# Routing rounds, order of GpSimd's work and buffers of weighted rows, moved in a fused attention and expert kernel

## Chip, cores and metric

One core of one Trainium2 chip. The metric is the device time of one execution in microseconds; lower is better. The median of three runs of the kernel before is 2441.61 us.

## What is computed

The input x is 32 x 512 x 256 in float32. The result is x + attention(layernorm(x)) + experts(layernorm(x)), cut to what matters:

```
xn  = layernorm(x)                                  # no scale, no shift
q, k, v = xn @ Wq + bq, xn @ Wk + bk, xn @ Wv + bv  # 16 heads of 16
a   = ((q k^T) * decay_mask) v                      # no softmax; mask 0.95^(i-j), causal
att = groupnorm(a @ Wo + bo) * gamma + beta         # 16 groups over channels and tokens

probs   = softmax(xn @ gate_w)                      # 8 experts
p, idx  = top_k(probs of each batch row and expert, 128)   # of its 512 tokens
h       = gelu(xn[idx] @ w1)                        # 256 -> 1024
y       = (h @ w2) * p                              # 1024 -> 256
out     = x + att + scatter_add(y at idx)
```

## The kernel before

The kernel has two blocks, one after the other, with a barrier between them. Every engine has its own program, and semaphores order them.

**Attention block.** It runs in passes b = -2 to 32 (B = 32 batch rows). Pass b does the front of row b + 1 (projections), the scores and values of row b and the output projection, group norm and residual of row b - 1; loads and layernorm run for row b + 2. In pass 32 only the tail of row 31 is left. SyncE stores the normalised rows xn (for the experts to gather) and x plus attention. GpSimd computes the group factors from VectorE's group means; ScalarE applies them, TensorE turns the rows back, and VectorE adds the residual.

**Routing.** The gate scores of two batch rows go through a softmax in 19 small VectorE steps, ten in the odd pass and nine in the even one that follows. Sixteen batch rows times eight experts make the 128 partitions of one half of the routing. For each half TensorE turns the scores (`turn_rows`), VectorE copies them (`take_rows`), and 16 rounds (`whole_round`: top eight, their index, strike them out) find the 128 best tokens. Then the indices are made float (`as_float`), TensorE turns values and indices (`turn_top`), and VectorE copies them out (`take_top`). The first half gets one round in each of the passes 16 to 31 and its top in pass 32. The second half is turned in pass 32, gets four rounds there, three before the first expert step, five after step 0 and four after step 1.

**Expert block.** It runs 64 steps, eight experts of NG = 8 steps, each with four batch rows (GRP = 4), so 512 gathered tokens. Numbers are split in a high and a low part, three matmuls for one product, and the first layer is done with seven products instead of eight. In a step n, TensorE runs products 6, 3 and 7 (x or sums of x times w1), the transposes of the rows gathered for step n + 1, products 1, 5 and 2 of step n + 1, and in between `down`, the second layer, four row blocks k of 24 matmuls. A step has 188 matmuls. ScalarE applies the gelu, makes high parts, and weights the second layer's result (`weighted`, L1272) into `y`, one buffer of four row blocks; its first one of a step waits until the scatter of the step before has landed. VectorE adds the products (L1429) and makes low parts (g_lo L1440, xs_lo L1399). `fronts(n + 1)` are the first hidden sums of the next step with a low part of x and of g between them, from the sum of product 2 to the sum called u4B.

GpSimd's turn for step n in order: gather of the rows of step n + 1 (four indirect DMAs, L1219, once the transposes of step n are through), scatter of step n - 1 (four indirect DMAs that add to the output, L1229), and, for the next expert, one weight sum (L1185 to L1191, in four turns), the low part of a slot of w1 (L1197) and of a piece of w2 (L1204). Both low parts wait for ScalarE's high part of the same piece, which comes late in the step. The instructions of each engine run strictly in this order.

## Time and profile before

| | |
|---|---|
| median of three runs | 2441.61 us (2440.53 to 2446.41) |
| profiled execution, its own time | 2432.42 us |
| its span | 2430.6 us |
| TensorE matmul busy | 2260.1 us, 93% |
| VectorE busy | 1625.8 us, 67% |
| ScalarE busy | 1383.7 us, 57% |
| GpSimd busy | 1243.0 us, 51% |
| mean granted TensorE clock | 0.978 |

In the rows below an instruction line gives start and duration in us, engine, line of the kernel, operation, out<-in, shape and count; in square brackets stands how long the engine was idle before it and what ended that. PE is TensorE, PEld its weight loads, DVE VectorE, ACT ScalarE, POOL GpSimd. The clock is the granted share of 2.4 GHz. A line of a group ends with busy time, mean ns of one, and idle time before them with what ended it.

### The profile page before, as it was taken

The numbers are of one execution on the slowest core, as the hardware profiler recorded it, in microseconds if no ns is written. First come the engines' busy times: TensorE is split into PE (matmuls) and PEld (weight loads), VectorE is DVE, ScalarE is ACT, GpSimd is POOL, SyncE is SP. The second block draws the span as 40 slices with busy tenths as digits, with TensorE's granted clock in tenths as the row PEclk, the third lists the DMA queues.
The fourth block names the chain that finished last, engine by engine and source line by source line (L and its number), as shares of the span: only waits on it lengthen the run. The fifth ranks groups of instructions, "written<-read, shape, count | busy, mean of one in ns | idle before, by whom it ended". The sixth has DMA issues, their size and how long they took to land.

```text
span 2430.6 us, 82507 instructions
## 1 busy us (share of the span) xinstructions
PE 2260.1 (93%) x34252; PEld 2076.0 (85%) x34252; DVE 1625.8 (67%) x3170; ACT 1383.7 (57%) x2545; POOL 1243.0 (51%) x2001
## 2 busy tenths in 40 slices
PE   6999999999999955799999999999999999999997
PEld 5777777777777745799999999999999999999997
DVE  2555555566666567777677777687686787777774
ACT  4555655655555524466566566566566666656664
POOL 4444444434544323356566566565565565665553
PEclk9999999999999977899999999999999999999998
DMA  3222222222223213133233233223233333332332
GB/s 98 81 90 73 82 89 81 73 88 90 74 73 98 64 45 87 27 44 85 47 44 83 47 46 84 47 45 81 42 51 77 48 51 75 53 49 47 53 53 26
DMA packets 129351, 157.58 MB, mean 65 GB/s; under 512 B 11008, under 2 KB 118656, under 8 KB 129024
## 3 DMA queue, kind: packets, MB, share of 16 engines
q0 software_dynamic: 49152, 67.14, 17.1%
q1 hardware_dynamic: 79872, 85.54, 11.3%
q8 instruction: 272, 4.46, 0.8%
q14 instruction: 55, 0.45, 0.1%
HBM read 85.53 MB, written 67.11 MB: 63 GB/s over the span
## 4 chain that ended last, share of the span: by engine, by line
PE 47%; DVE 4%; issue 3%; DMA 3%; ACT 2%; POOL 2%; ACTq 0%; another core or an unknown queue 0%; DVEq 0%; POOLq 0%
PE y L1604 24%; PE first_products_b L1536 7%; PE first_products_a L1536 6%; PE xt L1536 6%; PE fifth_products L1536 3%; DMA out<-y,scatter_idx 2%; PE xt L1526 2%; DVE g_lo L1440 1%; POOL out L1229 1%; ACT hidden L1310 1%; DVE hidden L1429 1%; POOL xg L1219 1%; DMA xg<-xn_rows,step_idx 1%; DVE xs_lo L1399 0%; ACT x_sums L1287 0%
## 5 line engine op out<-in xcount | busy, mean ns | idle before, releaser
L1604 PE MATMUL y<-w_hi,g_hi 128*128 128x256 f32 x2048 | 582.6, 284 | 24.4 <-ACT y L1272 17.2
L1604 PE MATMUL y<-w_lo,g_hi 128*128 128x256 f32 x2048 | 572.4, 279 | 0.0
L1604 PE MATMUL y<-w_hi,g_lo 128*128 128x256 f32 x2048 | 572.2, 279 | 0.0
L1229 POOL DMA_INDIRECT out<-y,scatter_idx x256 | 427.4, 1669 | 228.5 <-ACT y L1272 136.2
L1440 DVE TENSOR_TENSOR g_lo<-hidden,g_hi 128x512 fp32r<-128x512 f32 x512 | 422.6, 843 | 3.5 <-ACT g_hi L1314 1.2
L1604 PEld LDWEIGHTS y<-w_hi,g_hi 128*128 128x128 f32 x2048 | 389.1, 190 | 30.1 <-ACT y L1272 22.5
L1310 ACT ACTIVATE hidden<-hidden 128x512 f32<-128x512 f32 x384 | 236.7, 630 | 265.1 <-DVE hidden L1429 259.0
L1604 PEld LDWEIGHTS y<-w_lo,g_hi 128*128 128x128 f32 x2048 | 387.3, 189 | 0.0
L1604 PEld LDWEIGHTS y<-w_hi,g_lo 128*128 128x128 f32 x2048 | 386.9, 189 | 0.0
L1429 DVE TENSOR_TENSOR hidden<-xt,hidden 128x512 f32<-128x512 f32 x256 | 176.1, 688 | 250.9 <-PE xt L1536 238.7
L1219 POOL DMA_INDIRECT xg<-xn_rows,step_idx x256 | 262.6, 1026 | 115.1 <-issue 59.4
L1272 ACT ACTIVATE y<-y,top_p 128x256 f32<-128x256 f32 x256 | 121.0, 473 | 149.7 <-DMA out<-y,scatter_idx 93.5
L662 DVE TENSOR_TENSOR s_sb<-scores,cst 128x1024 f32<-128x1024 f32 x128 | 149.9, 1213 | 80.5 <-PE scores L875 80.5
L1204 POOL TENSOR_TENSOR w_lo<-w_stage,w_hi 128x256 fp32r<-128x256 f32 x56 | 41.4, 739 | 259.5 <-ACT w_hi L1325 259.5
L467 POOL TENSOR_TENSOR v_parity<-v_unbiased,bv_rows 128x256 f32<-128x256 f32 x128 | 92.2, 730 | 154.5 <-ACT v_unbiased L558 152.1
L1536 PE MATMUL first_products_a<-xs_hi,w_hi 128*128 128x256 f32 x512 | 147.1, 287 | 25.5 <-DVE hidden L1429 15.4
L1314 ACT ACTIVATE g_hi<-hidden 128x512 fp32r<-128x512 f32 x256 | 161.9, 633 | 6.2
L1429 DVE TENSOR_TENSOR hidden<-first_products_a,hidden 128x512 f32<-128x512 f32 x128 | 88.1, 689 | 97.8 <-PE first_products_a L1536 52.7
L1536 PE MATMUL first_products_b<-xs_hi,w_hi 128*128 128x256 f32 x512 | 144.6, 282 | 6.6 <-DVE hidden L1429 5.4
L1536 PE MATMUL first_products_b<-xs_hi,w_lo 128*128 128x256 f32 x512 | 143.2, 280 | 0.0
L1536 PE MATMUL first_products_a<-xs_lo,w_hi 128*128 128x256 f32 x512 | 143.0, 279 | 0.0
L1536 PE MATMUL first_products_a<-xs_hi,w_lo 128*128 128x256 f32 x512 | 143.0, 279 | 0.0
(190 smaller groups left out, 6182.3 us busy)
## 6 DMA issues: line engine op xcount, KB each, us to landing
x<-in_x SPq DMA_DIRECT2D x32, 512.0 KB, 5.2
w_stage<-in_w SPq DMA_DIRECT2D x16, 1024.0 KB
xn_rows<-xn SPq DMA_DIRECT2D x32, 512.0 KB, 3.2
res<-in_x SPq DMA_DIRECT2D x32, 512.0 KB, 3.8
out<-res SPq DMA_DIRECT2D x32, 512.0 KB, 3.5
xg<-xn_rows,step_idx POOLq DMA_INDIRECT x256
out<-y,scatter_idx POOLq DMA_INDIRECT x256
cst<-in_cst SPq DMA_DIRECT2D x1, 436.0 KB, 4.5
```

The lines of the kernel that those rows point to most:

```text
L467: pool.tensor_tensor(own, spread(vraw[:, t, 0:D]), spread(bv[:]), ALU.add).then_inc(vm_ready, 1)
L662: dve.tensor_tensor(s_sb[z][:, banks, :].rearrange("p k (g i) -> p (k g) i", i=SUB), sbk[:, banks, :].rearrange("p k (g i) -> p (k g) i", ...
L1219: pool.indirect_dma_start(xg[k][:], None, xn_d, bass.IndirectOffsetOnAxis(idx[:, k:k + 1], 0)).then_inc(gathered, 16)
L1229: pool.indirect_dma_start(out_rows, bass.IndirectOffsetOnAxis(sidx[:, k:k + 1], 0), y[:, k, :], None, compute_op=ALU.add).then_inc(scatter ...
L1272: act.activation(y[:, k, :], yb[k % 2][:, 0:D], ACT.Copy, scale=p_v[:, bass.ds(g * GRP + k, 1), bass.ds(e, 1)].rearrange("p a o -> p (a o) ...
L1310: act.activation(own(q, p), src, ACT.Gelu).then_inc(g_ready, 1)
L1314: act.activation(quadrant(g_hi, q, p), own(q, p), ACT.Copy).then_inc(gh_act, 1)
L1429: dve.tensor_tensor(dst, a, b, ALU.add).then_inc(sum_ready, 1)
L1440: dve.tensor_tensor(quadrant(g_lo, q, p), own(q, p), quadrant(g_hi, q, p).bitcast(F32), ALU.subtract).then_inc(gl_ready, 1)
L1526: last = pe.transpose(tb[:, h, k * P:(k + 1) * P], xg[k][:, h * P:(h + 1) * P], ident)
L1536: last = pe.matmul(dst, w_[par][:, w, cols], x__[:, x_, :], start=first and m == 0 and i == 0, stop=i == 2, skip_group_check=True)
L1604: last = pe.matmul(yb[k % 2][:, 0:D], g_[:, m, cols], w[n // NG % 2][:, m, :], start=start and m == first and i == 0, stop=end, skip_group ...
```

## The change

- The weighted rows go to two buffers in turn, the second of them the attention block's residual buffer; ScalarE waits for the scatter of two steps before (for step 1: until the attention block's last store has landed).
- GpSimd's turn n is now: scatter of step n - 1, gather of step n + 2, low part of w2 for the piece before, weight sum, low part of w1. The gather of step 1 is issued ahead of the first turn. The wait for the second half's indices moves from turn 3 to turn 2.
- The first half of the routing gets two rounds in the passes 20 and 25, so it is through in pass 29, and its top is taken in pass 30.
- Pass 31 does both parts of the last softmax ahead of its residuals, turns the second half's rows at its end and does two rounds; pass 32 does two after its first split, and three after the group means. Three more stand before the first expert step as before, and three in each of the steps 0 and 1, now ahead of `fronts`.
- ScalarE's inner loop over the steps of an expert is written out.

```diff
-    LAST_PASS_ROUNDS = 4
+    TWICE = (4, 9)
+    LAST_PASS_ROUNDS = (2, 2, 3)
-    STEP_ROUNDS = (5, 4)
+    STEP_ROUNDS = (3, 3)
...
+        TOP_AT = B - 2
...
+            def rounds(part):
+                n = Routing.LAST_PASS_ROUNDS
+                for r in range(sum(n[:part]), sum(n[:part + 1])):
+                    route.whole_round(dve, 1, r)
...
                 if has(a):
                     for s in range(2):
                         a_split(a, s)
+                if b == B:
+                    rounds(1)
...
-                if b == B:
+                if b == TOP_AT:
                     route.as_float(dve, 0)
-                    route.take_top(dve, 0, sbk[:, 0, :])
-                if b in (MID, B):
+                if b == MID:
                     softmax(b, par)
...
+                if b == TOP_AT:
+                    route.take_top(dve, 0, sbk[:, 0, :])
                 if b == B:
-                    route.take_rows(dve, 1, sbk[:, 2, :])
-                    for r in range(Routing.LAST_PASS_ROUNDS // 2):
-                        route.whole_round(dve, 1, r)
+                    rounds(2)
...
-                if 0 <= g < Routing.ROUNDS:
-                    route.whole_round(dve, 0, g)
+                if 0 <= g < TOP_AT - MID:
+                    r = g + sum(t < g for t in Routing.TWICE)
+                    route.whole_round(dve, 0, r)
+                    if g in Routing.TWICE:
+                        route.whole_round(dve, 0, r + 1)
...
+                if b == B - 1:
+                    softmax(b, par)
+                    softmax(B, 0)
                 if has(a):
                     for j in range(2):
                         residual(a, j)
-                if b not in (MID, B):
+                if b not in (MID, B - 1, B):
                     softmax(b, par)
                 if has(f):
                     states(f, fp)
-                if b == B:
-                    for r in range(Routing.LAST_PASS_ROUNDS // 2, Routing.LAST_PASS_ROUNDS):
-                        route.whole_round(dve, 1, r)
+                if b == B - 1:
+                    route.take_rows(dve, 1, sbk[:, 2, :])
+                    rounds(0)
...
+                    if b == TOP_AT:
+                        pe.wait_ge(route.chosen, 2)
...
-        y = sb("y", [P, GRP, D])
+        y = [sb("y", [P, GRP, D]), res]
...
             gather(0, 0, 0)
+            gather(0, 1, 1)
...
                 for g in range(NG):
-                    if first and g == NG // 2 - 1:
-                        pool.wait_ge(route.chosen, 4)
-                    if g < NG - 1:
-                        gather(e, g + 1, n0 + g + 1)
-                    elif not last:
-                        gather(e + 1, 0, n0 + NG)
                     if g:
                         scatter(e, g - 1, n0 + g - 1)
...
+                    if first and g == NG // 2 - 2:
+                        pool.wait_ge(route.chosen, 4)
+                    if g < NG - 2:
+                        gather(e, g + 2, n0 + g + 2)
+                    elif not last:
+                        gather(e + 1, g + 2 - NG, n0 + g + 2)
                     if g and not last:
                         if g == 1:
                             wait_apart(pool, w_in, 32 * e + 64, passed)
+                        else:
+                            low_w2(e, 1 - par, g - 1, g - 1)
                         if g <= 4:
                             weight_sum(e + 1, g)
                         low_w1(e, 1 - par, g)
-                        low_w2(e, 1 - par, g, g)
                 if not last:
+                    low_w2(e, 1 - par, NG - 1, NG - 1)
                     low_w2(e, 1 - par, 0, NG)
...
-                if k == 0:
-                    act.wait_ge(scattered, 16 * GRP * n)
+                if k == 0 and isinstance(n, int) and n == 1:
+                    act.wait_ge(out_stored, 16 * B)
+                elif k == 0 and not (isinstance(n, int) and n == 0):
+                    act.wait_ge(scattered, 16 * GRP * (n - 1))
...
-            def step(n, take, x_next):
+            def step(n, take, x_next, extra=(0, 0)):
...
                     x_sum(n + 1, 3)
+                    rounds(*extra)
                     fronts(n + 1)
...
             for n in range(Routing.TAKEN_AT):
-                step(n, False, True)
-                rounds(done, done + Routing.STEP_ROUNDS[n])
+                step(n, False, True, (done, done + Routing.STEP_ROUNDS[n]))
```

## Rows read from the trace of the kernel before

**Rows 1.** Busy time by stretch: us, PE, PEld, DVE, ACT, POOL, clock, DMA, GB/s.

```profile
100.00:863.95 763.95, 734.75 (x19917) 587.53 (x19905) 458.91 (x1108) 431.47 (x799) 339.99 (x1078) 1.00 0.26 80
863.95:921.12 57.17, 23.36 (x547) 18.48 (x547) 35.95 (x88) 12.06 (x13) 12.74 (x39) 0.62 0.22 66
921.12:1014.07 92.95, 63.48 (x476) 62.16 (x477) 72.84 (x167) 38.28 (x67) 31.13 (x29) 0.81 0.23 52
1014.07:2228.90 1214.83, 1174.68 (x9965) 1160.61 (x9965) 890.27 (x1484) 739.07 (x1372) 721.99 (x655) 0.99 0.32 57
2228.90:2381.38 152.48, 152.48 (x1319) 152.21 (x1318) 107.80 (x196) 95.59 (x172) 81.00 (x74) 1.00 0.31 49
```

**Rows 2.** Who waited for whom, 1014.07 to 2228.90 us: total, times, longest.

```profile
POOL w_lo L1204 <- ACT w_hi L1325: 248.4, 53, 7.4
...
ACT y L1272 <- DMA out<-y,scatter_idx: 82.4, 43, 5.7
...
PEld y L1604 <- ACT y L1272: 21.7, 15, 3.4
...
PEld xt L1526 <- DMA xg<-xn_rows,step_idx: 5.0, 6, 1.3
```

**Rows 3.** GpSimd's groups by form, 1014.07 to 2228.90 us.

```profile
L1229 POOL DMA_INDIRECT out<-y,scatter_idx x211 | 352.5, 1670 | 138.1 <-ACT y L1272 56.5 <-issue 53.6 <-POOL scatter_idx L1209 25.6
L1219 POOL DMA_INDIRECT xg<-xn_rows,step_idx x212 | 216.5, 1021 | 85.2 <-issue 49.3 <-POOL step_idx L1209 35.7 <-ACT y L1272 0.3
L1197 POOL TENSOR_TENSOR w_lo<-w_stage,w_hi 128x512 fp32r<-128x512 f32 x47 | 75.5, 1607 | 26.1 <-ACT w_hi L1320 25.8
L1204 POOL TENSOR_TENSOR w_lo<-w_stage,w_hi 128x256 fp32r<-128x256 f32 x53 | 39.2, 739 | 248.4 <-ACT w_hi L1325 248.4
L1191 POOL TENSOR_TENSOR w_stage<-w_stage 128x512 f32<-128x512 f32 x7 | 13.2, 1892 | 0.0
```

**Rows 4.** VectorE's groups by form, the same stretch.

```profile
L1440 DVE TENSOR_TENSOR g_lo<-hidden,g_hi 128x512 fp32r<-128x512 f32 x424 | 362.3, 871 | 2.5 <-ACT g_hi L1314 0.6
...
L1399 DVE TENSOR_TENSOR xs_lo<-x_sums,xs_hi 128x512 fp32r<-128x512 f32 x106 | 72.2, 681 | 0.0
```

**Rows 5.** ScalarE in order of time, around step 41.

```profile
1878.51 0.48 ACT L1272 ACTIVATE y<-y,top_p 128x256 f32<-128x256 f32 x1 [0.30 <-PE y L1604]
...
1893.46 0.47 ACT L1272 ACTIVATE y<-y,top_p 128x256 f32<-128x256 f32 x1 [4.24 <-DMA out<-y,scatter_idx]
```

**Rows 6.** GpSimd in order of time, the same step.

```profile
1882.70 1.63 POOL L1229 DMA_INDIRECT out<-y,scatter_idx  x1 [1.01 <-POOL scatter_idx L1209]
```

**Rows 7.** VectorE in order of time, an attention pass with a round.

```profile
589.96 0.69 DVE L675 TENSOR_TENSOR x_lo<-front,x_hi 128x512 fp32r<-128x512 f32 x1 [0.80 <-ACT x_hi L581]
```

**Rows 8.** VectorE in order of time, end of the attention block.

```profile
882.41 0.69 DVE L709 TENSOR_TENSOR res<-front,res 128x512 f32<-128x512 f32 x1 [0.16 <-PE front L974]
...
894.71 1.28 DVE L689 BATCH_NORM_STATS2 o_stats<-o 128x6 f32<-128x512 f32 x2
...
905.98 0.69 DVE L709 TENSOR_TENSOR res<-front,res 128x512 f32<-128x512 f32 x1 [0.16 <-PE front L974]
...
911.13 0.16 DVE L218 COPY topi<-best_index 128x8 uint32<-128x8 uint32 x1
```

**Rows 9.** VectorE in order of time, expert steps 0 to 2.

```profile
957.03 0.69 DVE L1429 TENSOR_TENSOR hidden<-xt,hidden 128x512 f32<-128x512 f32 x1 [4.27 <-PE xt L1536]
...
961.96 0.69 DVE L1429 TENSOR_TENSOR hidden<-first_products_b,hidden 128x512 f32<-128x512 f32 x1
...
975.38 0.68 DVE L1429 TENSOR_TENSOR hidden<-xt,hidden 128x512 f32<-128x512 f32 x1
...
991.91 0.69 DVE L1429 TENSOR_TENSOR hidden<-xt,hidden 128x512 f32<-128x512 f32 x1 [3.64 <-PE xt L1536]
...
997.33 0.68 DVE L1429 TENSOR_TENSOR hidden<-first_products_b,hidden 128x512 f32<-128x512 f32 x1
...
1009.61 0.68 DVE L1429 TENSOR_TENSOR hidden<-xt,hidden 128x512 f32<-128x512 f32 x1
```

44 lines of the change are left out of this document (23 added, 21 removed).

## Prediction

> **What bounds the kernel now.** I read the page first (busy shares, the forty slices), then busy time by stretch, then who waited for whom in the expert stage, then the engines in order of time at the places that the diff touches. Busy time by stretch [rows 1] splits the execution in five. In the attention passes and in the long expert stretch TensorE is busy 96 to 97% of the time at the full clock, so it bounds both. Between them lie two poor stretches: the end of the attention block (23.4 of 57.2 us busy, clock 0.62) and the first three expert steps (63.5 of 93.0 us, clock 0.81).
>
> The long stretch holds 53 expert steps (9965 matmul records at 188 a step): 1214.83 / 53 = 22.92 us each. The next seven steps, those of the last expert, in which no weights are prepared for a following one, take 152.48 / 7 = 21.78 us with no idle time at all [rows 1]. That is TensorE's own length of a step, the floor. So 1.14 us a step, 60.5 us in all, is lost to waits and to what they cost in clock (0.99). The waits [rows 2] name two causes directly: TensorE waits 21.7 us for ScalarE's weighted rows, which wait 82.4 us in 43 steps for the scatter of the step before to land, and 5.0 us for gathered rows. GpSimd itself waits 248.4 us in 53 steps for ScalarE's high part of w2, that is, at the end of every step, with the next gather and scatter queued behind it. In order of time: the fourth weighted rows are done at 1878.99 [rows 5], the scatter that sends them off starts only at 1882.70 [rows 6], and the next step's first weighted rows, which want the same buffer, start at 1893.46 after 4.24 us of waiting for its landing [rows 5].
>
> **The change, part by part. Two buffers for the weighted rows.** ScalarE now waits for the scatter of two steps before. A step's scatter has a whole further step of 21.8 us to land, so the 82.4 us of waiting go, and with them TensorE's 21.7 us.
>
> **GpSimd's order.** A turn is now scatter, gather for two steps on, low part of w2 for the piece before, weight sum, low part of w1. What a turn costs [rows 3]: a scatter instruction 1.67 us and (138.1 - 56.5) / 211 = 0.39 idle that is no wait for y, four times, 8.2 us; a gather 1.02 + 0.40, four times, 5.7; low parts 1.6 and 0.74; a weight sum 1.9 in four turns of an expert. That makes 18.1 us with a sum and 16.2 without, plus two small index copies, against 21.8 us of TensorE: GpSimd keeps up with about 3 us to spare. The high part of w2 that it used to wait for is by then one step old. The gather waits for the transposes of the step between; these are early in a step and the scatter ahead of it takes 8.2 us, so it lands more than ten microseconds before its rows are wanted, where before it was just in time; the 5.0 us go. Only the last two low parts of an expert still wait for ScalarE.
>
> **The low parts against VectorE.** VectorE's low parts of the activations take 871 ns on average, another subtraction of the same shape and also with both inputs in SBUF 681 ns [rows 4]; 0.19 us x 424 = 81 us are thus spent held up, and GpSimd's low parts take 1.6 us though they have only 512 columns [rows 3]. The new turn puts GpSimd's two-input operations about 14 to 18 us after the weighted rows, where VectorE waits for the second product anyway (3.6 to 4.3 us in the first steps [rows 9]). So I expect fewer collisions, not more, and with less held up VectorE the remaining waits of TensorE for hidden sums shrink too.
> The Trainium skill (SBUF — State Buffer, Who interferes with whom) says that a VectorE instruction with two SBUF inputs contends with a GpSimd instruction that reads SBUF, and that whichever starts first holds the shared pair for the whole instruction. By that rule a sum and a low part back to back can hold VectorE's subtraction for both their lengths wherever they fall, also at the newly exposed x part; the rival on collisions below is what this would be.
>
> **Size of the step term.** Bounds: nothing but the direct waits go, 21.7 + 5.0 = 26.7 us; or every step falls to the floor, 60.5 us. In between I take 21.9 us a step, nearer the floor, because it already holds in the seven steps where scatter and gather run as usual and only the weight work is missing, and ScalarE's share of that work is hidden by its idle time (739 of 1215 us busy [rows 1]): 1214.83 - 53 x 21.9 = **-54 us**.
>
> **Rounds in the first steps.** Before, five rounds stand between the end of the hidden sums at 962.65 and the next at 975.38, 12.7 us or 2.55 us a round, and four rounds and the float copies between 998.01 and 1009.61, 11.6 us [rows 9]. TensorE waits through most of both. Now the two steps get three rounds each, and ahead of the fronts, where VectorE is idle: free from 957.03 - 4.27 = 952.76, three rounds last until 960.4, 3.4 us past 957.03; in the second step from 988.27 until 995.9, 4.0 us past 991.91. From the first row of the fronts to the end of their last takes 5.6 and 6.1 us, for seven operations of 0.4 to 0.7, so one to two microseconds of waiting in them can absorb part. I take 2.5 and 3.0 late. The float copies (0.5) stay. 24.3 - 0.5 - 5.5 = 18.3, less 1 us should these shorter stalls still pull the clock down: **-17.3 us**, bounds -14 and -21.
>
> **End of attention.** The softmax halves move ahead of the last residuals of pass 31, into a wait, where the sixteenth round of the first half also used to stand. After the residual at 882.41 + 0.69 = 883.1 [rows 8] VectorE takes the rows (0.7 and up to 2 us for TensorE's transposes, I take 1), does two rounds (5.1), and only then the split of the attention output (1.3), which thus is several microseconds late and so is the output projection; two more rounds (5.1) run under the projection. The moments start at 896.3 instead of 894.71, where they had been held by softmax and copies: 1.6 late. From there the chain to the last residual is as before, so that ends at 906.67 + 1.6 = 908.3, with three rounds (7.7 us) in the wait for GpSimd's factors. Before, two rounds followed it and the block ended at 911.29 [rows 8]. **-3.0 us**, bounds 0 and -5; and seven rounds are done instead of four, which is what the first steps live on.
>
> **Attention passes.** Two passes get a second round of 2.55 us. After a round VectorE waits 0.80 us for ScalarE [rows 7] and again before the residuals, so most is hidden: 0.3 to 1 us each (if nothing hid it, 2.55 each). Taking the first half's top eight in pass 30 adds two transposes on TensorE and two short copies on VectorE, 0.5 us at most. **+1 us**, bounds 0 and +5. ScalarE's unrolled steps cost nothing that I can see: it is 61% busy in this stretch. In the last steps ScalarE's same wait goes: **-1 us**.
>
> **Sum:** +1 - 3.0 - 17.3 - 54 - 1 = -74.3 us. The profiled execution has a span of 2430.6 us (its own time is 2432.4) and the median of the runs is 2441.6, 9 us above it; I take the difference as it is: span 2356.3, median 2367.3, called 2367 us.
>
> **Rivals.**
> *Only the direct waits go.* VectorE, not ScalarE, is then what holds the fronts of a step, and TensorE's remaining 18 us of waits for hidden sums and low parts (1214.83 - 1174.68 = 40.2 us idle less 21.7) stay with their clock. For it: some steps without any scatter wait lie above the floor. Against: VectorE is 73% busy. Step term -26.7, time 2394.6.
> *Collisions move instead of going.* The sum and low part (1.9 + 1.6 us) hit the x part or the first low part of the fronts in four steps of eight, 26 steps; about 1 us left of each after slack: +26, time 2393.
> *The rounds stay exposed.* Three rounds ahead of the fronts delay the sixth product and the split waits at the end of attention, and both give back what they won: +20.3, time 2387.
> *GpSimd becomes the bound* (the other side). The gather is now behind the scatter in every turn. If instructions slow each other so that a turn passes 21.8 us, TensorE follows GpSimd's turn; slower than before in all from a turn of (1214.83 + 20.3) / 53 = 23.3 us, 5 us above my sum of 18.1. At 24 us: 53 x 24 - 1214.83 = +57, with the other terms +37, time 2478. Against: it needs every instruction a quarter longer than its mean.
>
> **Chances.** Forecast 0.69; only direct waits 0.14; collisions 0.08; rounds exposed 0.06; GpSimd bound 0.03. The forecast's own range is 2352 to 2382. The range goes to 2350 (all terms at their good ends make -86) and up to 2395, over the first three rivals. Within 0.3% (7 us), about what a measurement of this kernel can tell from no change, I give 0.02 for a mix of these, out of the forecast's share; faster 0.95, slower 0.03.
>
> **What would show it.** ScalarE's wait for the scatter gone from the waits; GpSimd's w2 low part waiting about once or twice an expert; seven-step groups of 21.8 to 22.0 us; the mean of VectorE's g_lo nearer 700 ns; clock 1.00 in the long stretch; the first three steps some 75 us long instead of 93; seven rounds before the expert block. It would be wrong if GpSimd is above 85% busy with gathers that TensorE waits for, if new waits for xs_lo appear at the sixth product in every other step, or if the passes with two rounds are over 1 us longer.

## The result, and the profile of the changed kernel

The changed kernel takes 2341.6 us (median of 4 runs, 2337.92 to 2344.88); the kernel before, run beside it, 2441.07 us (4 runs, 2439.77 to 2446.41). The ratio is 0.9588, 95% interval 0.9568 to 0.9609: 99.5 us less. The forecast of 2367 us had the direction and the mechanism, but the time fell below its range (2350 to 2395).

Busy time by stretch of the changed kernel, with the columns of [rows 1]: from 863.95 us to the first transposes of the expert block, the first three expert steps, the 53 steps after them, seven of the last expert's steps.

```profile
863.95:919.11 55.16, 22.18 (x545) 17.54 (x545) 41.68 (x104) 12.06 (x13) 12.80 (x39) 0.67 0.26 78
919.11:992.21 73.10, 61.38 (x476) 60.20 (x477) 64.58 (x144) 38.17 (x67) 27.81 (x26) 0.87 0.25 62
992.21:2142.84 1150.63, 1150.63 (x9966) 1150.63 (x9965) 810.22 (x1484) 744.89 (x1373) 750.44 (x658) 1.00 0.34 61
2142.84:2294.81 151.97, 151.97 (x1318) 151.97 (x1317) 107.06 (x196) 95.53 (x172) 83.27 (x75) 1.00 0.31 50
```

In the third line TensorE's busy time is the whole stretch. It does not wait once in 53 steps; 1150.63 / 53 = 21.71 us a step, and the seven steps behind it take the same 151.97 / 7 = 21.71. Against [rows 1], in us:

| stretch | before | after | difference | forecast |
|---|---|---|---|---|
| start to first transposes | 921.12 | 919.11 | -2.0 | +1 - 3 = -2 |
| expert steps 0 to 2 | 92.95 | 73.10 | -19.9 | -17.3 |
| 53 steps | 1214.83 | 1150.63 | -64.2 | -54 |
| 7 steps and the end | 201.7 | 200.2 | -1.5 | -1 |
| span | 2430.6 | 2343.0 | -87.6 | -74.3 |

So 13 us of the miss of 25 us are in the terms, 10 of them in the step term. The other 12 are between the two profiled executions and the medians (87.6 against 99.5), which is taken up below.

Who waited for whom in the 53 steps (engine and line, what released it; total us, times, longest):

```profile
DVE hidden L1454 <- PE xt L1561: 231.4, 53, 4.4
...
POOL out L1251 <- ACT y L1299: 144.2, 27, 8.3
POOL out L1251 <- ACT res L1299: 117.8, 26, 6.4
```

Two kinds of row that led [rows 2] are gone: GpSimd's 248.4 us for ScalarE's high part of w2 (1.1 us are left), and ScalarE's 82.4 us for the scatter. Their place is taken by GpSimd waiting for the weighted rows (262 us in the 53 steps). That idleness does no harm: GpSimd is early, and it waits for the rows that it sends off next. GpSimd's groups in the same stretch, to be held against [rows 3]:

```profile
L1241 POOL DMA_INDIRECT xg<-xn_rows,step_idx x212 | 230.3, 1086 | 85.9 <-issue 50.3 <-POOL step_idx L1231 35.6
L1251 POOL DMA_INDIRECT out<-y,scatter_idx x107 | 183.7, 1717 | 168.6 <-ACT y L1299 144.2 <-issue 21.3 <-PE xt L1551 3.0
L1251 POOL DMA_INDIRECT out<-res,scatter_idx x106 | 182.0, 1717 | 142.1 <-ACT res L1299 117.8 <-issue 21.3 <-PE xt L1551 3.0
L1219 POOL TENSOR_TENSOR w_lo<-w_stage,w_hi 128x512 fp32r<-128x512 f32 x47 | 60.9, 1295 | 0.0
L1226 POOL TENSOR_TENSOR w_lo<-w_stage,w_hi 128x256 fp32r<-128x256 f32 x53 | 39.4, 746 | 2.1 <-ACT w_hi L1351 1.1
...
L1213 POOL TENSOR_TENSOR w_stage<-w_stage 128x512 f32<-128x512 f32 x7 | 9.1, 1300 | 0.0
```

A low part of w1 takes 1295 ns and no longer 1607, a weight sum 1300 and no longer 1892. VectorE's side of it, against [rows 4]:

```profile
L1465 DVE TENSOR_TENSOR g_lo<-hidden,g_hi 128x512 fp32r<-128x512 f32 x424 | 281.1, 683 | 1.8
...
L1424 DVE TENSOR_TENSOR xs_lo<-x_sums,xs_hi 128x512 fp32r<-128x512 f32 x106 | 72.9, 688 | 0.0
```

The 0.19 us by which g_lo was longer than its like is gone. It was a mean: before, 376 of the 424 took under 0.85 us and 48 took 1.5 to 4.1 us; now the longest takes 0.70. One turn of GpSimd in order of time (start, length, engine, operation, and in brackets the idle time before it):

```profile
1790.80 1.62 POOL L1251 DMA_INDIRECT out<-y,scatter_idx  x1 [5.24 <-ACT y L1299]
...
1799.67 1.46 POOL L1241 DMA_INDIRECT xg<-xn_rows,step_idx  x1 [0.93 <-POOL step_idx L1231]
...
1805.16 0.76 POOL L1226 TENSOR_TENSOR w_lo<-w_stage,w_hi 128x256 fp32r<-128x256 f32 x1
1805.87 1.30 POOL L1219 TENSOR_TENSOR w_lo<-w_stage,w_hi 128x512 fp32r<-128x512 f32 x1
...
1812.51 1.62 POOL L1251 DMA_INDIRECT out<-res,scatter_idx  x1 [3.35 <-ACT res L1299]
```

The turn lasts 21.71 us (1790.80 to 1812.51), starting from a wait. In [rows 5] and [rows 6] the scatter began 4.2 us after the start of the fourth weighted rows; here it begins 1.3 us after the start of the rows that it sends off (1789.48, below). Those rows of before lie at a change of expert, where it was latest. Counted from the end of the fourth weighted rows, the scatters of the 53 steps began 0.80 to 6.12 us later before, 1.90 in the mean; now it is 0.80 to 0.86 us in every step. The four scatters take 7.7 us, the weight work falls between 1805 and 1809, and 3.35 us are left over. ScalarE in order of time, the last weighted rows of one step in the one buffer and the first of the next step in the other. Where [rows 5] had 4.24 us of waiting, the second has no bracket at all, though the scatter of the first buffer has barely been issued:

```profile
1789.48 0.47 ACT L1299 ACTIVATE y<-y,top_p 128x256 f32<-128x256 f32 x1 [0.29 <-PE y L1629]
...
1800.16 0.48 ACT L1299 ACTIVATE res<-y,top_p 128x256 f32<-128x256 f32 x1
```

VectorE in order of time at the end of attention, against [rows 8]. Two rounds of the routing stand ahead of the low parts of the attention output and two behind it (885 to 890 and 891 to 896), then the moments, then three rounds in the wait for GpSimd's factors:

```profile
884.59 0.69 DVE L195 COPY rows<-scores 128x512 f32<-128x512 f32 x1
...
889.94 1.28 DVE L670 TENSOR_TENSOR a_lo<-attn,a_hi 128x512 fp32r<-128x512 f32 x2
...
908.06 0.69 DVE L711 TENSOR_TENSOR res<-front,res 128x512 f32<-128x512 f32 x1 [0.16 <-PE front L991]
```

The last residual ends at 908.75 (forecast: 908.3), where the block of before went on to 911.29. The same engine in the second expert step, against [rows 9]: the last x sum, three rounds from 950.63 to 957.68 (2.35 us each), then the fronts, and TensorE's wait at that place.

```profile
950.29 0.41 DVE L1434 TENSOR_TENSOR x_sums<-xt,x_sums 128x256 f32<-128x256 f32 x1
950.63 0.68 DVE L203 MAX8 best<-rows 128x8 f32<-128x512 f32 x1
...
957.68 0.68 DVE L1454 TENSOR_TENSOR hidden<-xt,hidden 128x512 f32<-128x512 f32 x1
```
```profile
959.11 0.36 PE L1561 MATMUL first_products_a<-xs_hi,w_hi 128*128 128x256 f32 x1 [0.65 <-DVE xs_lo L1424]
```

In the third step the same place costs TensorE 2.99 us, followed by 3.41 us at the lower clock level, 1.2 GHz. The steps are 22.68 and 26.65 us long. There are three rounds again. What differs is one copy (128x8) in the first of them, which takes 0.16 us in the other five (VectorE, then GpSimd at the same time):

```profile
975.36 2.49 DVE L217 COPY top<-best 128x8 f32<-128x8 f32 x1
```
```profile
975.26 1.29 POOL L1207 TENSOR_TENSOR w_stage<-w_stage 128x512 f32<-128x512 f32 x1
976.51 1.29 POOL L1219 TENSOR_TENSOR w_lo<-w_stage,w_hi 128x512 fp32r<-128x512 f32 x1
```

It starts with GpSimd's weight sum and ends 0.05 us after the low part that follows. That is 2.33 us, the whole difference between a stall of 2.99 and one of 0.65 us: GpSimd's first weight work meets VectorE here.

### The profile page after: what moved, and what is told of

Its sections match the earlier page's. It is cut to its first block, busy times and chain, and to the rows that moved or that the text cites. A ratio compares the mean times of both kernels' runs of the same rounds, so it can differ in the third digit from the quotient of the medians.

```text
span 2343.0 us, 81527 instructions
## 1 busy us (share of the span) xinstructions
PE 2234.4 (95%) x34252; PEld 2063.7 (88%) x34252; DVE 1543.0 (66%) x3170; ACT 1389.9 (59%) x2545; POOL 1272.7 (54%) x2001
## 4 chain that ended last, share of the span: by engine, by line
PE 58%; DVE 2%; issue 0%; ACT 0%; POOL 0%; DMA 0%; DVEq 0%; POOLq 0%
PE y L1629 29%; PE first_products_a L1561 8%; PE first_products_b L1561 8%; PE xt L1561 7%; PE fifth_products L1561 4%; PE xt L1551 2%; DVE best_index L207 0%; POOL out L1251 0%; DVE best L203 0%; DMA w_stage<-in_w 0%; DVE xs_lo L1424 0%; DVE rows L211 0%; DVE g_lo L1465 0%; DVE x_sums L1434 0%; DVE top L217 0%
## 5 line engine op out<-in xcount | busy, mean ns | idle before, releaser
L1629 PE MATMUL y<-w_hi,g_hi 128*128 128x256 f32 x2048 | 576.0, 281 | 0.0
L1465 DVE TENSOR_TENSOR g_lo<-hidden,g_hi 128x512 fp32r<-128x512 f32 x512 | 339.4, 683 | 2.2
L1241 POOL DMA_INDIRECT xg<-xn_rows,step_idx x256 | 276.9, 1082 | 116.4 <-issue 61.1
L1251 POOL DMA_INDIRECT out<-y,scatter_idx x128 | 219.4, 1714 | 221.2 <-ACT y L1299 192.0
L1251 POOL DMA_INDIRECT out<-res,scatter_idx x128 | 219.1, 1712 | 190.9 <-ACT res L1299 161.7
L426 POOL TENSOR_SCALAR ln_ve<-ln_mv 128x4 f32<-128x4 f32 x32 | 7.4, 231 | 251.1 <-DVE ln_mv L642 251.1
L1561 PE MATMUL xt<-xs_hi,w_hi 128*128 128x256 f32 x512 | 142.8, 279 | 0.0
```

What stands on the lines that cost most here:

```text
L426: pool.tensor_scalar(ln_ve[:], mv[:, :, 1], EPS, None, ALU.add).then_inc(ln_chain, 1)
L1241: pool.indirect_dma_start(xg[k][:], None, xn_d, bass.IndirectOffsetOnAxis(idx[:, k:k + 1], 0)).then_inc(gathered, 16)
L1251: pool.indirect_dma_start(out_rows, bass.IndirectOffsetOnAxis(sidx[:, k:k + 1], 0), y[g % 2][:, k, :], None, compute_op=ALU.add).then_inc( ...
L1465: dve.tensor_tensor(quadrant(g_lo, q, p), own(q, p), quadrant(g_hi, q, p).bitcast(F32), ALU.subtract).then_inc(gl_ready, 1)
L1561: last = pe.matmul(dst, w_[par][:, w, cols], x__[:, x_, :], start=first and m == 0 and i == 0, stop=i == 2, skip_group_check=True)
L1629: last = pe.matmul(yb[k % 2][:, 0:D], g_[:, m, cols], w[n // NG % 2][:, m, :], start=start and m == first and i == 0, stop=end, skip_group ...
```

## Experiments

Twelve kernels in three series, on three chips, each timed beside the kernel before on the same chip: its medians were 2437.99, 2440.79 and 2436.95 us. Kernels of different series are best compared by their ratios to before. "53 steps" is the stretch from step 3 on, cut at the same instructions in every kernel; it stands at 1214.83 us before and 1150.63 us after.

**The kernel before, once more.** No edit. What does one profiled execution of it stand for?

> The kernel before, unchanged, profiled and timed again. The changed kernel's profiled execution is 87.6 us shorter in its span than the profiled execution of before (2343.0 against 2430.6), but the medians of the runs differ by 99.5 us. Theory: the steps of before wander from execution to execution (stalls of TensorE of 1 to 4 us, some followed by a stretch at half clock), and the execution that was profiled was a lucky one; then the spans of other executions are 2435 to 2446 us at a slightly lower clock, and the extra time lies in the expert steps. Rival: the profile shifts all kernels by about the same, and the 12 us are something between the blocks; then spans of unprofiled executions stand 9 us from the profiled one at the same clock.

2440.71 us (10 runs, 2435.68 to 2444.6), ratio 1.001 [0.9994, 1.0026]. The profiled execution was a long one this time, span 2442.8 us:

```profile
925.77:1019.01 93.24, 64.09 (x476) 62.83 (x477) 72.83 (x167) 38.48 (x67) 31.08 (x29) 0.81 0.22 52
1019.01:2241.36 1222.35, 1176.73 (x9966) 1162.33 (x9966) 891.19 (x1484) 738.52 (x1372) 723.67 (x655) 0.99 0.31 57
```

The 12.2 us over the first profile are 4.65 up to the first transposes and 7.5 in the 53 steps: the theory holds for the larger part, and the rest lies ahead of the expert block. Over all series 49 executions of this kernel took 2427.95 to 2446.41 us, median about 2439. The profile that I had forecast from was thus short by some 7 to 9 us, where there is most to lose: in the steps.

**The two buffers alone.** Of before:

```diff
-        y = sb("y", [P, GRP, D])
+        y = [sb("y", [P, GRP, D]), res]
...
-                if k == 0:
-                    act.wait_ge(scattered, 16 * GRP * n)
+                if k == 0 and isinstance(n, int) and n == 1:
+                    act.wait_ge(out_stored, 16 * B)
+                elif k == 0 and not (isinstance(n, int) and n == 0):
+                    act.wait_ge(scattered, 16 * GRP * (n - 1))
...
-                with act.Fori(1, NG - 1 if last else NG) as g:
+                for g in range(NG):
```

> Before, with only the second buffer of weighted rows (and ScalarE's steps written out, which it needs); GpSimd's order and the routing as before. Theory A (the scatter's landing was the cause of the stalls): ScalarE's wait for the scatter goes and the step term is nearly all there, -45 to -60 us. Theory B (GpSimd's place in its own turn was the cause): ScalarE's waits go, but the gathered rows stay just in time and VectorE's low parts stay held up (mean of g_lo still near 870 ns), so steps stay 0.4 to 0.8 us above 21.71 and the gain is 20 to 40 us.

2417.34 us (2411.68 to 2423.2), ratio 0.9927 [0.9893, 0.996]. By stretch, by wait and by group:

```profile
1015.46:2215.53 1200.07, 1168.44 (x9965) 1156.51 (x9965) 907.34 (x1484) 736.49 (x1372) 730.81 (x655) 1.00 0.32 58
```
```profile
POOL w_lo L1204 <- ACT w_hi L1326: 239.5, 53, 7.3
...
PEld y L1604 <- DVE g_lo L1440: 21.2, 20, 1.7
```
```profile
L1440 DVE TENSOR_TENSOR g_lo<-hidden,g_hi 128x512 fp32r<-128x512 f32 x424 | 374.7, 900 | 2.5 <-ACT g_hi L1316 0.6
```

ScalarE's wait for the scatter is gone (0.1 us left) and TensorE's for ScalarE's rows with it. But the 53 steps lose only 14.8 us of the 64.2: GpSimd is still late at the end of every turn (239.5 us), g_lo is still held up (900 ns), and TensorE's weight loads wait 21.2 us for g_lo, where it was 6.2 before. Taking away the wait that the profile names moved the stall to another one. This is theory B, with less gain than it said (20 to 40 us): a step is still 0.93 us above the floor.

**GpSimd's order alone**, with one buffer and ScalarE as before: the lines of the diff in gpsimd's program and nothing else.

```diff
             gather(0, 0, 0)
+            gather(0, 1, 1)
...
+                    if g < NG - 2:
+                        gather(e, g + 2, n0 + g + 2)
...
+                        else:
+                            low_w2(e, 1 - par, g - 1, g - 1)
```

> Before, with only GpSimd's order (scatter, gather two steps on, low part of w2 one piece behind, sum, low part of w1); one buffer of weighted rows, ScalarE's loop kept, the routing as before. Theory A: ScalarE must still wait for a landing, 8 us of issue plus 2 to 4 of flight after the fourth weighted rows, so 1 to 3 us of wait in every step and TensorE held by about 1 us in most: gain 0 to 30 us. Theory B: scatters start 3 us earlier, ScalarE's waits stay under what TensorE notices, g_lo's mean falls to 0.69 us, and steps stand at 21.71 to 21.9: gain 50 to 65 us.

2367.96 us (2364.87 to 2371.94), ratio 0.9724 [0.9687, 0.976].

```profile
1011.49:2163.60 1152.11, 1151.11 (x9966) 1150.71 (x9965) 813.10 (x1484) 749.46 (x1373) 743.82 (x655) 1.00 0.33 60
```
```profile
ACT y L1275 <- DMA out<-y,scatter_idx: 40.7, 50, 1.9
```

Theory B, and nearly all of the step term: 21.74 us a step, 1.5 us in all above the floor. Of these, 1.3 us are in step 3, behind the late rounds of before; the 52 steps from there on take 1129.07 us, and 1128.92 in the changed kernel. ScalarE still waits 0.8 us a step for the scatter, and TensorE does not notice. The parts do not add: 14.8 and 62.7 are 77.5 us, and only 64.2 were to be had.

**The routing alone**: all of the diff in the attention passes, the first steps and TensorE's part of the routing, on the kernel before.

```diff
-    LAST_PASS_ROUNDS = 4
+    LAST_PASS_ROUNDS = (2, 2, 3)
...
-    STEP_ROUNDS = (5, 4)
+    STEP_ROUNDS = (3, 3)
...
                     x_sum(n + 1, 3)
+                    rounds(*extra)
                     fronts(n + 1)
```

> Before, with only the routing's change (two double rounds, top in pass 30, seven rounds by the end of pass 32, three and three ahead of the fronts); buffer and GpSimd's order as before. Theory: as in the changed kernel's trace, the expert block starts 2 us earlier and the first three steps take about 74 instead of 93 us: gain 20 to 23 us. Rival: part of the 20 us came from gathers two steps ahead and from GpSimd's order in the first steps; then the gain here is 12 to 17 us.

2411.79 us (2407.39 to 2416.84), ratio 0.9908 [0.9875, 0.994], which is 22 us; 20 to 23 were expected. The first three steps take what they take in the changed kernel, the 53 behind them 1214.16 us, as before. In GpSimd's old order the first weight work meets a g_lo (2.92 us) and not the copy, and the stall of the third step is as long, 2.96 us.

```profile
919.03:992.60 73.57, 61.49 (x477) 60.16 (x477) 65.35 (x144) 37.82 (x67) 29.00 (x28) 0.87 0.26 62
```

The medians of this run and of the order alone are 26.2 and 70.0 us below before's; the sum, 96.2, is 3 us short of the 99.5 of the whole change. By the ratios the two give only 22 and 67 us, which leaves about 10, so such sums can't price the second buffer. The stretches can: in the steps from 4 on it is worth 0.2 us beside the order (above), and from the end of the 53 steps to the end of the kernel 0.8 us (200.98 us with the order alone, 200.2 with both). A kernel with everything but the second buffer was not run.

**Collisions without lateness.** In the changed kernel the weight work moves ahead of the gather:

```diff
                         scatter(e - 1, NG - 1, n0 - 1)
-                    if first and g == NG // 2 - 2:
...
                         low_w1(e, 1 - par, g)
+                    if first and g == NG // 2 - 2:
```

> The changed kernel with one thing moved: GpSimd's weight work (low part of w2 one piece behind, weight sum, low part of w1) stands between scatter and gather instead of behind the gather, so it falls 5 to 6 us earlier, while VectorE makes the low parts of g. No wait is added except for ScalarE's high part of w1. Theory collisions (what held the steps of before was VectorE held up by GpSimd's two-input operations): g_lo's mean goes from 683 ns to 800 to 900 ns, steps go from 21.71 to 22.0 to 22.6 us, 15 to 45 us slower than the changed kernel. Theory lateness (the steps were held by scatters and gathers that started late): scatter still starts as soon as y is ready, so 0 to 5 us slower, whatever g_lo's mean does.

2350.35 us (2347.53 to 2351.8), ratio 0.9632 [0.9613, 0.9651].

```profile
990.46:2147.00 1156.54, 1153.80 (x9967) 1151.97 (x9966) 884.43 (x1484) 733.13 (x1373) 778.67 (x658) 1.00 0.33 60
```
```profile
L1465 DVE TENSOR_TENSOR g_lo<-hidden,g_hi 128x512 fp32r<-128x512 f32 x424 | 355.2, 856 | 1.8
```

Earlier in a turn (7.0 us after the start of the scatter, where it was 14.4) the weight work meets the low parts of the activations: g_lo takes 856 ns, nearly as in [rows 4], VectorE is 74 us busier, and yet the steps lose just 5.9 us, most of it in two waits of TensorE (2.7 us) with 3.4 us at the lower clock. That is just above the 0 to 5 us of theory lateness and far from the 15 to 45 of theory collisions; in the ratios the kernel is 9 to 11 us slower than the changed one, of which the steps explain 5.9. So collisions cost little at this place, where GpSimd is on time. They can cost more: with the two buffers alone, g_lo at 900 ns and GpSimd late, TensorE waits for g_lo. No run has the lateness without any collisions.

**The lateness alone.** In the kernel before, only the low part of w2 is made one piece behind, so that it no longer waits within an expert; the order of gather and scatter and the single buffer stay:

```diff
+                        else:
+                            low_w2(e, 1 - par, g - 1, g - 1)
...
                         low_w1(e, 1 - par, g)
-                        low_w2(e, 1 - par, g, g)
                 if not last:
+                    low_w2(e, 1 - par, NG - 1, NG - 1)
```

> Before, with only the low part of w2 taken one piece behind, so that GpSimd no longer waits for ScalarE at the end of a turn; gather of the next step, then scatter, then weight work, one buffer, the routing as before. Theory lateness: the 248 us of GpSimd's waits for the high part of w2 go, scatters start as soon as y is ready, and steps fall to 21.7 to 22.0 us: gain 45 to 62 us, as with the whole order. Theory collisions: the weight work still falls right behind the scatter, on VectorE's low parts of g: g_lo's mean stays at 800 ns or more and steps stay above 22.2 us, gain under 35 us.

2391.55 us (2387.93 to 2394.84), ratio 0.9805 [0.9785, 0.9826].

```profile
1014.72:2183.78 1169.06, 1157.00 (x9965) 1152.69 (x9965) 882.21 (x1484) 738.57 (x1372) 763.97 (x654) 1.00 0.33 59
```
```profile
L1442 DVE TENSOR_TENSOR g_lo<-hidden,g_hi 128x512 fp32r<-128x512 f32 x424 | 353.7, 852 | 2.4 <-ACT g_hi L1316 0.6
```
```profile
1507.17 0.47 ACT L1274 ACTIVATE y<-y,top_p 128x256 f32<-128x256 f32 x1 [5.07 <-DMA out<-y,scatter_idx]
```

Without the wait at the end of most turns 45.8 of the 64.2 us are gained, with g_lo as slow as ever (852 ns). What is left, 18.4 us, sits mostly at the change of expert: the first two steps of the six experts in this stretch are 14.8 us above the floor in all (the longest takes 25.06 us), with waits like that of the last row above. The cause is the same as in the other turns of before. The last two low parts of an expert still wait for ScalarE, with gather and scatter behind them (GpSimd, ahead of the row above):

```profile
POOL w_lo L1204 <- ACT w_hi L1327: 36.4, 12, 5.3
```
```profile
1486.04 0.73 POOL L1204 TENSOR_TENSOR w_lo<-w_stage,w_hi 128x256 fp32r<-128x256 f32 x1 [5.25 <-ACT w_hi L1327]
...
1495.48 1.63 POOL L1229 DMA_INDIRECT out<-y,scatter_idx  x1 [1.01 <-POOL scatter_idx L1209]
```

Here the fourth weighted rows were done at 1491.77, so the scatter is 3.7 us late. Put side by side: how late the scatter starts (from the end of the fourth weighted rows, mean of the 53 steps, and in how many it is over 1.5 us), g_lo's mean, and the time of the steps.

| kernel | scatter starts, us | over 1.5 us | g_lo, ns | 53 steps, us |
|---|---|---|---|---|
| before | 1.90 | 28 | 871 | 1214.83 |
| two buffers alone | 2.35 | 32 | 900 | 1200.07 |
| low part of w2 one piece behind, alone | 1.19 | 7 | 852 | 1169.06 |
| weight work ahead of the gather | 0.83 | 0 | 856 | 1156.54 |
| order alone | 0.82 | 0 | 690 | 1152.11 |
| changed | 0.83 | 0 | 683 | 1150.63 |

Two kernels with g_lo at 852 and 856 ns, hardly less than before, are 45.8 and 58.3 us faster, and both have their scatters on time in most or all steps. The two buffers gain their 14.8 us with the scatters later than ever. The landing plays no part: where ScalarE waited for one, it went on 2.2 to 3.6 us after the end of the fourth issue (median 2.5), before, with the order alone and in this kernel alike.

**The wait put back, behind everything.** In the changed kernel the low part of w2 is again that of the step's own piece, last in its turn:

```diff
-                        else:
-                            low_w2(e, 1 - par, g - 1, g - 1)
...
                         low_w1(e, 1 - par, g)
+                        low_w2(e, 1 - par, g, g)
                 if not last:
-                    low_w2(e, 1 - par, NG - 1, NG - 1)
```

> The changed kernel with the low part of w2 as before: last in GpSimd's turn, of this step's piece, waiting for ScalarE's high part. Scatter first and gather two steps on stay. The high part is ready some 16 us after the fourth weighted rows and GpSimd gets there at 15 to 18. Theory (not GpSimd's wait is the cost, but the gather that stood ahead of the scatter behind it): steps stay at 21.7 to 21.8 us, 0 to 4 us slower than the changed kernel. Rival (the wait is the cost; taking it away alone gave 46 of the 63 us): steps rise to 22 us or more, over 15 us slower.

2338.43 us (2335.47 to 2345.5), ratio 0.9602 [0.9576, 0.9628], against 2338.65 us of the changed kernel on the same chip.

```profile
985.66:2136.29 1150.63, 1150.63 (x9966) 1150.63 (x9965) 809.78 (x1484) 744.30 (x1373) 749.68 (x658) 1.00 0.34 61
```
```profile
POOL w_lo L1226 <- ACT w_hi L1349: 2.9, 6, 1.1
```

No difference. With the scatter first and the gather behind it, a turn reaches this instruction about when ScalarE has made its high part, and the wait of 248.4 us [rows 2] is 2.9 us. "One piece behind" and "scatter first, gather two ahead" both remove the lateness; the second does it in every turn and makes the first needless. What a long wait behind the scatter would cost this run can't tell, because none came up, and scatter first and gather two ahead were not tried apart.

**The rounds behind the fronts.** In the changed kernel:

```diff
                     x_sum(n + 1, 3)
-                    rounds(*extra)
                     fronts(n + 1)
+                    rounds(*extra)
```

> The changed kernel with the three rounds of the steps 0 and 1 behind the fronts of the next step, where before had its five and four. Theory: all six rounds then stand where VectorE has no idle time and TensorE needs its next sum: of six times 2.45 us the stalls take 14.7 less the 2 to 3 us that TensorE has in hand each time, so 7 to 11 us slower than the changed kernel, in steps 1 and 2 alone. Rival: the place is worth little and the gain came from nine rounds becoming six; then under 3 us slower.

2356.06 us (2352.03 to 2358.08), ratio 0.9651 [0.9631, 0.9672].

```profile
918.82:1002.99 84.17, 64.49 (x477) 63.35 (x478) 65.50 (x145) 38.27 (x67) 30.60 (x28) 0.83 0.25 57
```

The stretch is 11.1 us longer, with two stalls of 5.55 and 5.59 us (0.65 and 2.99 in the changed kernel) and two falls to the lower clock of 6.83 us each, which begin before the stalls are over; step 3, too, takes 22.96 instead of 21.71 us. With it the cost is 12.3 us, a little over the 7 to 11 that were expected. So of the 19.9 us of this stretch about 11 come from the place of the rounds and the rest from there being six instead of nine.

**The first rounds split**: in the changed kernel one of the three first rounds stays ahead of the x sums and two go in front of fronts(0).

```diff
-            rounds(sum(Routing.LAST_PASS_ROUNDS), done)
+            rounds(sum(Routing.LAST_PASS_ROUNDS), done - 2)
...
             x_sum(0, 3)
+            rounds(done - 2, done)
             fronts(0)
```

> The changed kernel with the three rounds ahead of the first expert step split: one stays ahead of the sums of x, two go behind them, ahead of the first fronts, where VectorE stands idle for 5.6 us until product 2 is through. In the changed kernel's trace the x sums start 4.9 us after ScalarE has the first copy. Theory: the first product starts 4.6 us earlier and the two rounds (4.9 us) fit into the idle time: 4 to 5 us faster than the changed kernel. Rival: the first fronts then wait for the rounds as the later ones do, and TensorE's clock rises no earlier: 0 to 2 us faster.

2339.29 us (2335.49 to 2342.67), ratio 0.9582 [0.956, 0.9604]; the stretch is 5.3 us shorter than in the changed kernel, where 4 to 5 were expected. The times do not show it: the interval of the ratio overlaps those of the changed kernel (0.9568 to 0.9617 in its two timings), and this execution reached the first transposes late, at 921.83.

```profile
921.83:989.61 67.78, 60.05 (x476) 59.12 (x477) 64.63 (x144) 38.04 (x67) 28.57 (x26) 0.91 0.28 67
```

**The changed kernel again, and the rounds in every gap.** The first has no edit. The second has four first rounds, one of them between the low parts of the first weights, and two instead of three in the third step:

```diff
-    FIRST_ROUNDS = 3
-    STEP_ROUNDS = (3, 3)
+    FIRST_ROUNDS = 4
+    STEP_ROUNDS = (3, 2)
...
+                if i == 2:
+                    rounds(sum(Routing.LAST_PASS_ROUNDS), sum(Routing.LAST_PASS_ROUNDS) + 1)
...
-            rounds(sum(Routing.LAST_PASS_ROUNDS), done)
+            rounds(sum(Routing.LAST_PASS_ROUNDS) + 1, done - 2)
...
             x_sum(0, 3)
+            rounds(done - 2, done)
             fronts(0)
```

> The changed kernel, unchanged, once more, on the same chip as the three that follow. Theory (the kernel before wanders by the stalls of its steps, the changed one does not have them): its expert steps 3 to 62 take 21.71 us each in every execution, and its executions spread by no more than the attention block does, within 8 us, against 2428 to 2446 us of before. Rival: the spread is the same and the steps of before only looked unlucky.

> The changed kernel with the last nine rounds laid into VectorE's gaps: one between the low parts of w1 and of w2 at the start of the expert block (a gap of 2.4 to 2.7 us), one behind them, two ahead of the first fronts, then three in step 0 and two in step 1. Steps from 3 on are as in the changed kernel. Theory: the first round is hidden whole, the first x sums come 4.6 us earlier, and the stall of 3 us in step 2, with the half clock behind it (together 4.9 us above a full step), shrinks to under 1.5 us: the stretch from the first transposes to step 3 goes from 73.1 to 64 to 65 us, 8 to 9 us faster than the changed kernel. Rival: the round in the gap delays the low part of w2 and the second layer of step 0 waits for it: 4 to 6 us faster only.

The changed kernel: 2338.65 us (2335.79 to 2340.23), ratio 0.9597 [0.9577, 0.9617], steps 0 to 2 in 72.85 us and the 53 steps in 1150.62. Its four executions spread over 4.4 us and those of the first timing over 7.0, within the 8 us of the theory; those of the run above, with the same steps, over 10.0. The other: 2333.0 us (2326.43 to 2334.28), ratio 0.9565 [0.9543, 0.9588].

```profile
917.15:981.36 64.21, 59.21 (x477) 57.95 (x477) 61.73 (x137) 38.04 (x67) 26.91 (x25) 0.93 0.27 69
```

The stretch is 8.6 us shorter; the stalls in its second and third step are 0.66 and 0.60 us and the clock no longer falls behind them. The held copy is still there, 2.48 us long; the stall of 0.60 us comes from one round less. In the medians 5.65 us remain: this execution reached the first transposes 5 us later than its neighbour (917.15 against 912.11). It is the fastest version of the study, though the intervals of the two ratios still touch.

**ScalarE's steps written out, alone**: in the kernel before the inner loop of its program is unrolled, as the two buffers require.

```diff
-                with act.Fori(1, NG - 1 if last else NG) as g:
-                    step(n0 + g, (e, g), (e, g - 1), None if last else (e, 1 - par, g), True)
+                for g in range(NG):
...
```

> Before, with only ScalarE's inner loop written out. Theory: ScalarE is 61% busy and waits in every step, so a branch per step costs nothing: within 3 us of before. Rival: the branch delays ScalarE's first instruction of each step and part of the gain of the two buffers alone (which needed it) comes from here: 5 to 15 us faster.

2434.45 us (10 runs, 2429.38 to 2443.14), ratio 0.9992 [0.9978, 1.0006]; 53 steps in 1220.06 us, within what before itself shows (1214.2 to 1222.4). The cost of nothing at which I put it stands.

## Why the prediction was right in kind and too careful in size

**The step that failed is "Size of the step term": 21.9 us a step, -54 us.** Measured are 21.71 and -64.2 us, beyond even the bound of -60.5. The bound was wrong because the floor was a mean of seven steps, 152.48 / 7 = 21.78. Step by step in the same trace of before, the first two of the seven took 21.93 and 21.98 us and the other five 21.71 to 21.73, although no wait of TensorE shows in them. The 0.1 us a step that I added was an allowance for collisions and for a ScalarE at times late; neither costs TensorE anything in the changed kernel. So the mechanism was right and this term of the sum was too small by 10.2 us.

**"I take the difference as it is" failed with it.** The forecast carried one profiled execution's distance to the median over to the changed kernel. But that execution was short for its kernel by some 9 us, and a good part of the spread of before is in steps that wait (1214.2 to 1222.4 us in four profiles with this GpSimd program); the changed kernel's steps took 1150.62 or 1150.63 in each of its two profiles. The profiled execution of before lies 8.7 us below the median (2432.4 to 2441.1), that of the changed kernel, the longest of four, 3.3 above it (2344.9 to 2341.6). That is 12 us of the miss; the terms are the other 13.

**Two buffers: "the 82.4 us of waiting go, and with them TensorE's 21.7 us"** was right as to the waits and wrong as to their worth. Alone they give 14.8 us in the steps; beside the order 0.2 us in the steps from 4 on and 0.8 at the end. I had read the most visible wait as a cause; it was the effect of a scatter issued late.

**GpSimd's order** was right, and is nearly the whole: 62.7 us alone. The sum of a turn holds: four scatters at 1.717 + 0.30 are 8.1 us, four gathers at 1.086 and 85.9 / 53 idle 6.0, low parts 2.0, a sum 1.3, the two index copies 1.1, together 18.5 us with a weight sum (forecast 18.1 and the copies) and 17.2 without (16.2 and the copies). The agreement is in part luck: the sum and the low part are 0.9 us shorter than put down, the copies, which were named but not priced, 0.6 us longer than the 0.5 us of before. GpSimd's three microseconds to spare are seen as 3.35 us of waiting in the turn shown. The experiments put the cause where [rows 2] have their largest entry: a wait at the end of each turn, with the gather and the scatter of the next queued behind it. Without it in most turns, 45.8 us of the 64.2 go; most of the rest is the same wait at the change of expert, which the new order no longer lets stand ahead of the scatter.

**The low parts against VectorE**: g_lo fell to 683 ns as forecast, and the rival of collisions (+26 us, with the Trainium skill's rule beside it, SBUF — State Buffer, Who interferes with whom, that the first to start holds the shared pair for its whole length) was tried: with weight work in the wrong place g_lo is at 856 ns and the steps lose 5.9 us, 4.4 times less than priced. The trace of that run agrees with the rule (VectorE, then GpSimd):

```profile
1563.43 2.75 DVE L1465 TENSOR_TENSOR g_lo<-hidden,g_hi 128x512 fp32r<-128x512 f32 x1
```
```profile
1562.49 1.89 POOL L1213 TENSOR_TENSOR w_stage<-w_stage 128x512 f32<-128x512 f32 x1
1563.74 1.88 POOL L1219 TENSOR_TENSOR w_lo<-w_stage,w_hi 128x512 fp32r<-128x512 f32 x1
```

The held g_lo ends 0.56 us after the second of GpSimd's instructions, and 47 of the 48 that took over 0.85 us end 0.55 or 0.56 us after one. What I had overrated is the way to TensorE: VectorE waits 183 us for it in these steps in any case (131.5 and 51.9). One collision does reach TensorE in the changed kernel. It is between a round and the weight work of step 1 and was in no rival; it costs 2.3 us and, to judge by the shorter stalls, the fall of the clock in the third step.

**Rounds in the first steps**: -19.9 against -17.3. A round takes 2.41 to 2.43 us and not 2.55; the five rounds of before had a held copy (0.93 us) among them. The sum's parts are off in both directions. TensorE's stalls at the two places went from 11.28 and 9.90 us (below) to 0.65 and 2.99, so 17.5 us less and not 18.3: the forecast took VectorE's 24.3 us for TensorE's loss. And the clock, which was to cost 1 us, gave about 2 back: before, 3.44 and 4.32 us of TensorE's work ran at 1.2 GHz behind these stalls, now 3.41 us in the third step alone, and half of that time is lost at half the clock (an estimate). The 3.0 us put down for the third step were met by luck: without the held copy the estimate is 2.99 - 2.33 = 0.7.

```profile
976.72 0.58 PE L1536 MATMUL first_products_a<-xs_hi,w_hi 128*128 128x256 f32 x1 [11.28 <-DVE hidden L1429]
...
1009.75 0.47 PE L237 MATMUL fifth_products<-cst,top 128*128 128x128 f32 x1 [9.90 <-DVE rows L230]
```

**Attention**: the sum of its two terms, -2.0, is what was measured, and the last residual came 0.4 us after its forecast. This is worth little as a check, though: over the profiles of this study the first transposes lay between 911.8 and 925.8 us, so a term of 2 us there can't be read from one. The medians point the same way: 918.0 us over the eight profiles with the new attention passes, 921.6 over the six with the old. The passes with two rounds did show the sign of being wrong that was named, over 1 us longer (from VectorE's first low part in pass 20 to that in pass 21 it takes 28.4 us, 27.2 before), but the next pass is as much shorter (25.2 against 26.7), and the pair of pass 25 is alike, so hardly any of it stays.

The other rivals fell plainly: the direct waits were not the whole (26.7 us against 64.2), the rounds are not exposed, and GpSimd is 65% busy in the long stretch and far from bounding it.

Not settled: why the attention block wanders by up to 14 us in all kernels, how much of the gain scatter first has without gather two ahead, and by which way the late scatters reached TensorE in the kernel before, through the landing that ScalarE waits for (removing that wait alone gave 14.8 us) or through weight work that then falls on a g_lo that TensorE wants at once.

## What to carry to other kernels

A wait in an in-order queue costs what is queued behind it: price it not by who waits for its result but by the urgent work that follows it, and first try to move that work ahead of it. A second buffer for a late consumer does little until the consumer is on time, and next to nothing afterwards (here 1 us). Read a floor from single undisturbed steps, not from the mean of a quiet stretch, and place the one profiled execution among several timed ones before carrying its distance to the median over to another kernel.

## What the runs showed of the hardware

- A TensorE stream that never waits is exact: 53 steps of 188 matmuls took 1150.62 or 1150.63 us in five profiles of four kernels. The wander is where something waits.
- Two-input operations of GpSimd and VectorE that meet lengthen each other: GpSimd's 128x512 low part from 1295 to 1592 ns and its 128x256 one from 746 to 1201, a 128x512 weight sum from 1300 to 1892, VectorE's g_lo from 683 to 900 on average. A held g_lo goes on until 0.55 us after the end of GpSimd's instruction, or of the next one that follows without a gap, up to 4.3 us in all. VectorE's sums with one input in PSUM stayed at 685 to 692 ns on average in all of these kernels.
- A copy of 128x8 values on VectorE is held up in the same way: 2.49 us instead of 0.16 beside a weight sum and a low part of GpSimd.
- The landing of the indirect scatters varies little: in three kernels with one buffer, ScalarE, where it waited for one, went on 2.2 to 3.6 us after the end of the fourth issue, 2.5 in the median. It waited 0.8 us a step where the scatter was issued on time and up to 5.7 us where it was issued late.
- Stalls of TensorE of 0.60 to 0.66 us left the clock alone; behind one of 2.99 us it stood at 1.2 GHz for 3.41 us, at ones of 5.55 and 5.59 us for 6.83 us each. The length of the stall does not decide it alone: 2.90 us with the low part of w2 one piece behind was followed by no fall (clock 1.00), 1.74 us with ScalarE's steps written out by one of 3.41 us.
